# Two gated transformer blocks on one core: one region of 1024 slot rows per expert, and a new order around the routing

## The chip, the cores and the metric

The kernel runs on one core of a Trainium2 chip. The metric is the device time of one execution in microseconds (us). The engines of the core are named as in the profile: PE is TensorE (PEld its weight loads), DVE VectorE, ACT ScalarE, POOL GpSimd and SP SyncE, which here only issues DMAs.

## What is computed

The input is 2 batches of 512 tokens with 256 features. Cut to what matters:

```
xn = layernorm(x)
s  = attention0(xn)                     # 16 heads, 4 key/value heads, rotary
g  = silu(ffn0(xn))                     # gate/up/down, inner size 1024
x  = x + s * g
xn = layernorm(x)
# branch: linear attention
Q, K, V = split(xn @ W_in.T + b_in)     # 256 -> 768
Q, K = rope(Q), rope(K)
A  = sum over tokens of (K / |K|) * V   # one row per batch
s  = (A * Q) @ W_out.T + b_out + xn
# experts: top-1 of 8
route = sigmoid(xn @ router_w); e = argmax(route); prob = max(route)
g  = silu(prob * (silu(xn @ gate_w[e]) * (xn @ up_w[e])) @ down_w[e])
x  = x + s * g
```

## The kernel before

Token tiles have 128 tokens: 8 in all (NT), 4 per batch (TB). Each engine runs its own instruction list in order, and semaphores tie the lists together.

**Attention part.** A planner, `attention_plan`, writes one list of items (scores, row maxima, probabilities, values, and the gate, up and down products of block 0 as filling), and every engine walks that list for its own share. Small steps are put at a step and quarter by `due(step, quarter, item)`; a small cost table (`Clock.PE`, `other`) decides how much filling goes in front of an item whose inputs it believes late. Batch 0 gets its second layernorm, the transposes `rows_T` and its router logits inside this part (steps 19 to 22), batch 1 at its end. PSUM bank 5 (`misc`) is shared by the small steps through the semaphore `misc_free`. The list ends with the products `qkv1` of W_in for the four tiles of batch 0, with `rope1(0)` and with the logits of batch 1.

**Routing.** After the list DVE routes all 8 tiles at once (L1181 to L1216): probability, one-hot, a running sum over tiles, and after two PE products ("counts", L1559 and L1560) the row of every token. Token rows are packed: an expert starts at the first tile after the previous expert's last one, so the row of any token depends on the totals of all 1024. Then POOL scatters the 8 token tiles into DRAM (`xs_dram`, "slot_rows", 15 x 128 rows) with 8 indirect DMAs (L779). At its start SP has filled this area once with rows that carry no token (`in_empty`).

**Expert tiles.** SP waits for all 8 scatters and loads 8 slot tiles, one DMA each with a fixed address (L677), then releases the weights of experts 0 to 2, which it had loaded before, and issues the loads of experts 3 to 7 (L687). PE's `tile(i)` reads the expert's number from `tile_e`, makes the gate (L1600), the transposes of the tile before (L1576), up (L1608), the transposes of the next slot rows (L1568) and the down product of the tile before (L1586). The inputs need 11 expert tiles. ACT makes the tanh of each tile (L960), copies transposes out of PSUM (L942, L948) and DVE multiplies (L1279, L1283, L1270, L1273). POOL scatters each result.

**Branch.** Between the plan and the first expert tile PE makes the W_in products of batch 1 (L1382; bank pair 6 and 3 in turns, freed by DVE's bias addition L1035), the transposes of Q (`q_T`, L1622, copied out by ACT L936), the token sum of batch 0 (L1631) and `branch(0)`, `branch(1)` (L1643). `side_work(i)` puts the rest behind expert tiles 0 to 3: key norms and token sum of batch 1, `branch(2)`, `branch(3)`. ACT's squares of the keys (L862) wait for the rotation of their batch. `keep_warm` are transposes without use.

## Time and profile before

| | us |
|---|---|
| median of 3 runs | 370.25 |
| lowest, highest | 370.02, 370.71 |
| span of the profiled execution | 370.6 |
| PE busy in it | 326.3 (88%) |
| DVE busy | 239.2 (65%) |
| ACT busy | 154.4 (42%) |
| POOL busy | 62.8 (17%) |

The profiled execution has a span of 370.6 us and nothing is reported around it, so it stands 0.35 us above the median. Times in the text are counted from the start of the span. The span has three parts: the attention part up to about 250, the stretch between it and the first expert tile (250 to 280.5), and the expert tiles with the output (280.5 to the end). A row of the chain of waits is one piece of the work that ended last; a row of the timeline is one or a few instructions of an engine, with the idle time before them and what ended it in brackets.

### The profile page before, as it was taken

The page shows a single profiled execution, that of the slowest core. Times are in us where ns is not written, and L with a number is a line of the kernel's source. Part 1 is how long each engine was busy: PE and PEld are TensorE (multiplying, and loading weights), DVE is VectorE, ACT ScalarE, POOL GpSimd, SP SyncE. Part 2 cuts the span into 40 slices and gives each one's busy share as a digit, 9 for nine tenths or more (in the row PEclk, how much of TensorE's full clock was granted, in tenths as well). Part 3 has the DMA queues.
Part 4 walks back from the last instruction along what each step waited for, and adds up shares of the span by engine and source line. Part 5 has one row for each costly group of instructions (what it writes and reads, how often), then busy time and mean ns, then how long its engine had stood idle before and what let it go on. Part 6 is the DMA issues. An engine that isn't in the chain of part 4 may idle for free.

```text
span 370.6 us, 4637 instructions
## 1 busy us (share of the span) xinstructions
PE 326.3 (88%) x1598; PEld 191.5 (52%) x1598; DVE 239.2 (65%) x473; ACT 154.4 (42%) x279; POOL 62.8 (17%) x64
## 2 busy tenths in 40 slices
PE   3849859999999999999999999989968999999730
PEld 3426636545555454455554555556554576666420
DVE  3999895977666677877958510499793644433305
ACT  1614722476766655553664555203113322332300
POOL 4372480000011000000000000014570111211211
PEclk9958997999999999999999999996998999999965
DMA  7960000000000000000000050093029960111015
GB/s 262 405 161 0 2 0 3 0 3 1 0 4 0 3 0 3 0 0 3 2 2 1 0 171 2 2 371 138 31 92 329 435 240 30 30 42 44 17 44 200
DMA packets 9914, 28.46 MB, mean 77 GB/s; under 512 B 1342, under 2 KB 6559, under 8 KB 8608
## 3 DMA queue, kind: packets, MB, share of 16 engines
q1 hardware_dynamic: 8976, 26.01, 19.3%
q0 software_dynamic: 912, 2.12, 1.5%
q8 instruction: 15, 0.25, 0.3%
q14 instruction: 11, 0.09, 0.1%
HBM read 24.86 MB, written 5.55 MB: 82 GB/s over the span
## 4 chain that ended last, share of the span: by engine, by line
PE 72%; DVE 17%; DMA 4%; issue 2%; POOL 2%; ACT 1%; DVEq 0%; SPq 0%; POOLq 0%
PE ps L1532 11%; PE ps L1477 8%; PE ps L1445 8%; PE ps L1545 7%; PE ps L1467 7%; PE ps L1586 6%; PE ps L1600 6%; PE ps L1608 5%; PE ps L1382 3%; DVE xn L1014 3%; PE ps L1407 2%; DVE nmax L1069 2%; POOL slot_rows L779 2%; PE ps L1361 2%; PE ps L1576 1%
## 5 line engine op out<-in xcount | busy, mean ns | idle before, releaser
L1069 DVE TENSOR_REDUCE nmax<-ps 128x1 f32<-128x512 f32 x128 | 85.8, 688 | 34.4 <-PE ps L1445 33.7
L880 ACT ACTIVATE shared<-ps 128x512 f32<-128x512 f32 x128 | 74.2, 594 | 53.9 <-PE ps L1467 52.8
L1445 PE MATMUL ps<-experts 96*128 96x512 bf16 x128 | 48.2, 384 | 1.8 <-DVE experts L1076 1.2
L1467 PE MATMUL ps<-experts 99*128 99x512 bf16 x128 | 48.5, 382 | 0.0
L1545 PE MATMUL ps<-shared,experts 128*128 128x256 f32 x128 | 38.0, 386 | 0.0
L1477 PE MATMUL ps<-shared,experts 128*32 128x512 f32 x256 | 34.1, 605 | 0.3 <-ACT shared L880 0.3
L1445 PEld LDWEIGHTS ps<-experts 96*128 96x128 bf16 x128 | 12.5, 98 | 36.8 <-DVE nmax L1069 18.2
L1545 PEld LDWEIGHTS ps<-shared,experts 128*128 128x128 f32 x128 | 23.3, 191 | 9.7 <-issue 3.4
L1382 PE MATMUL ps<-late_weights,xnT 128*128 128x512 f32 (+1 forms) x64 | 25.0, 542 | 0.7 <-DVE shared L1035 0.7
L769 POOL TENSOR_TENSOR experts<-experts,late_weights 128x768 f32<-128x768 f32 x1 | 1.8, 1809 | 130.9 <-ACT experts L870 130.9
L888 ACT ACTIVATE experts<-ps 96x1024 bf16<-96x1024 bf16 x18 | 18.0, 1020 | 12.5 <-PE ps L1407 12.4
L1586 PE MATMUL ps<-experts,shared 128*128 x88 | 22.5, 402 | 0.8 <-ACT shared L948 0.8
L1600 PE MATMUL ps<-experts,xsT 128*128 x44 | 22.1, 627 | 0.7 <-ACT xsT L942 0.7
L1608 PE MATMUL ps<-experts,xsT 128*128 x44 | 20.7, 593 | 0.0
L1532 PE MATMUL ps<-xnT,late_weights 128*128 128x512 f32 x48 | 19.6, 407 | 0.0
L1382 PEld LDWEIGHTS ps<-late_weights,xnT 128*128 128x128 f32 x64 | 13.1, 213 | 10.6 <-issue 8.8
L1586 PEld LDWEIGHTS ps<-experts,shared 128*128 128x128 f32 x88 | 16.9, 203 | 3.1 <-issue 1.0
L1467 PEld LDWEIGHTS ps<-experts 99*128 99x128 bf16 x128 | 12.4, 98 | 9.9 <-issue 3.5
L1279 DVE SCALAR_TENSOR_TENSOR gated<-tanh_g,ps 128x512 f32<-128x512 f32 x11 | 7.6, 687 | 13.1 <-ACT tanh_g L960 13.1
L1128 DVE SCALAR_TENSOR_TENSOR gx<-gated,ps 128x256 f32<-128x256 f32 x8 | 3.4, 421 | 18.5 <-ACT gated L917 18.4
L1344 PE MATMUL ps<-wl,xnT 128*128 128x384 f32 x32 | 12.7, 557 | 1.8 <-DVE xnT L1028 1.2
L954 ACT ACTIVATE late_weights<-late_weights 128x256 f32<-128x256 f32 x11 | 4.6, 417 | 22.9 <-DVE late_weights L1270 22.9
(204 smaller groups left out, 536.3 us busy)
## 6 DMA issues: line engine op xcount, KB each, us to landing
experts<-in_experts SPq DMA_DIRECT2D x8, 1536.0 KB, 10.6
shared<-in_wgu SPq DMA_DIRECT2D x1, 2048.0 KB, 11.1
slot_rows<-in_empty SPq DMA_DIRECT2D x1, 1950.0 KB, 19.6
late_weights<-slot_rows SPq DMA_DIRECT2D x9, 130.0 KB, 2.3
x<-in_x SPq DMA_DIRECT2D x2, 512.0 KB, 5.7
shared<-in_wdn SPq DMA_DIRECT2D x1, 1024.0 KB, 13.1
shared<-expert_results SPq DMA_DIRECT2D x4, 256.0 KB, 3.7
out_x<-x SPq DMA_DIRECT2D x4, 256.0 KB, 2.0
```

The costliest lines, as they stand in the source:

```text
L880: nc.scalar.activation(probs[:, n % 2, hh, :], ps[:, 2 + hh % 2, :], ACT.Exp, scale=float(HD) ** -0.5).then_inc(s["exp_done"], 1)
L888: nc.scalar.activation(dst, src.rearrange("p (h s) -> p h s", h=2), ACT.Copy).then_inc(s["misc_free" if b else "stack_copied"], 1)
L1069: nc.vector.tensor_reduce(nmax[:, 4 * t + hh:4 * t + hh + 1], ps[:, m % 2, :], AX, ALU.max, negate=True).then_inc(s["max_done"], 1)
L1382: last = nc.tensor.matmul(bank[:, a, 0:hi - lo], xnT[:, k, P * j:P * j + P], win[:, k, lo:hi], start=k == 0, stop=k == KD - 1)
L1445: nc.tensor.matmul(ps[:, m % 2, :], qs[0:KS, b, GR * g + hh, P * t:P * t + P], ks[0:KS, b, g, :], start=True, stop=True).then_inc(s["score ...
L1467: nc.tensor.matmul(ps[:, 2 + hh % 2, :], ks[0:KM, b, g, P * t:P * t + P], qs[0:KM, b, GR * g + hh, :], start=True, stop=True).then_inc(s[" ...
L1477: last = nc.tensor.matmul(ps[VW * hh:VW * hh + VW, 4, :], vaug[:, TB * b + t, g, :], probs[:, n % 2, hh, :], start=t == 0, stop=t == TB - 1)
L1532: ins = nc.tensor.matmul(ps[:, bk, :], w_parts[w_], x_parts[x_], start=k == 0 and n_ == 0, stop=k == KD - 1 and n_ == 2)
L1545: ins = nc.tensor.matmul(ps[:, bk, 0:D], hT[:, i, P * (j % TB):P * (j % TB) + P], wdn[:, i, :], start=i == 0, stop=i == NI - 1)
L1586: last = nc.tensor.matmul(ps[:, 6, 0:D], hmT[:, i % 2, P * k:P * k + P], Wm[:, bass.ds(base[i] + 2 * KD * EI + D * k, D)], start=k == 0, s ...
L1600: last = nc.tensor.matmul(ps[:, i % 2, :], xsT[:, i % 2, P * k:P * k + P], Wm[:, bass.ds(base[i] + EI * k, EI)], start=k == 0, stop=k == K ...
L1608: last = nc.tensor.matmul(ps[:, 2 + i % 2, :], xsT[:, i % 2, P * k:P * k + P], Wm[:, bass.ds(base[i] + EI * (KD + k), EI)], start=k == 0, ...
```

## The change

- `xs_dram` grows to 8 regions of 1024 rows, one per expert (8192 rows). A token's row is its expert's region plus the tokens of that expert before it, so batch 0 needs nothing of batch 1. It is routed (`route`, three stages), counted (`counts`) and given rows (`place_rows`) at steps 23 and 24 of the attention part, and POOL scatters its 4 tiles then. The empty rows are written in four DMAs of 2048 rows, each after the row-maxima DMAs of one of the first four units.
- After the plan only batch 1 is routed: 4 tiles, with the totals of batch 0 as its start. PE's counts come one W_in product earlier (after tile 4, not after tile 5). The last step of `rope1(0)` moves behind the routing on DVE. DVE now makes the rows, then all tables of tiles (14 instructions, two tables more: `tile_r` is the first slot row of each expert tile), and only then the bias addition of tile 4.
- POOL makes the second scatter before the product of keys and values and the key norms of batch 0.
- SP reads `tile_r` into a register for each slot tile and loads the rows at this address. It waits for the tables and the scatters; slot tiles 3 to 7 wait for the last W_in product (all waited for it before).
- PE makes the fourth W_in product of batch 1 straight after the third, then `q_T(0)` and `q_T(1)`. `q_T(2)`, `q_T(3)` and the token sum of batch 0 go behind expert tile 0, `branch(0)` behind tile 1, `branch(1)` and the token sum of batch 1 behind tile 2, `branch(2)` behind tile 3, `branch(3)` behind tile 4. `q_T(2)` and `q_T(3)`, the token sums and all branches use PSUM bank 7; `q_T(3)` waits until ACT has copied `q_T(2)`.
- ACT makes the squares of batch 1's keys and the last two Q copies after the tanh of tile 0. DVE adds up the tokens of batch 0 (`sum_tiles(0)`) and scales W_out (`scaled_output(0)`) in tile 0, does the key norms of batch 1 in tile 1.

```diff
-SLOTS = MT * P
+REGION = TOK
+SLOTS = E * REGION
+EMPTYINGS = 4
...
-                           (21, 2, ("rows_T", 0, 0)), (22, 0, ("rows_T", 0, 1)), (22, 2, ("logits", 0))):
+                           (21, 2, ("rows_T", 0, 0)), (22, 0, ("rows_T", 0, 1)), (22, 2, ("logits", 0)),
+                           (23, 1, ("route", 0, 0)), (23, 3, ("route", 0, 1)), (24, 1, ("route", 0, 2)), (24, 3, ("counts", 0)),
+                           (24, 3, ("place", 0))):
...
-    return {0: [("norm", 1)], 1: [("sum", 1)], 2: [("branch", 2)], 3: [("branch", 3)]}.get(i, [])
+    return {0: [("squares", 1), ("sum_tiles", 0), ("q_T", 2), ("q_T", 3), ("sum", 0)], 1: [("norm", 1), ("branch", 0)],
+            2: [("branch", 1), ("sum", 1)], 3: [("branch", 2)], 4: [("branch", 3)]}.get(i, [])
...
             def load_rows(i):
-                sp.dma_start(slot_row(i), xs_dram[P * i:P * i + P, :]).then_inc(x_sem[i % XR], 16)
+                row = sp.value_load(tile_r[0:1, i:i + 1], min_val=0, max_val=SLOTS - P)
+                sp.dma_start(slot_row(i), xs_dram[bass.ds(row, P), :]).then_inc(x_sem[i % XR], 16)
...
+                    sp.wait_ge(s["tile_experts"], 1)
                     sp.wait_ge(s["scattered"], 16 * NT)
-                    sp.wait_ge(s["qkv1_psum"], NT)
                     for i in range(XR):
+                        if i == 3:
+                            sp.wait_ge(s["qkv1_psum"], NT)
                         load_rows(i)
                     for a in range(FIRST_EXPERTS):
                         expert_here(a)
...
+            scatter(0)
             pool.wait_ge(s["qkv1_copied"], 1)
             pool.wait_ge(s["layer1_loaded"], 64)
             nc.gpsimd.tensor_tensor(qkv1[0][:, 1, :], qkv1[0][:, 1, :], bin_b, ALU.add).then_inc(s["bias_added"], 1)
             pool.wait_ge(s["bias_added"], 1)
+            scatter(1)
             key_times_value(0)
...
+            def place_rows(b, bank, read):
+                dve.wait_ge(s["counts"], b + 1)
...
+                nc.vector.tensor_copy(smi[:, TB * b:TB * b + TB], at8).then_inc(s["slots"], 1)
+                if b == 0:
+                    nc.vector.tensor_copy(small[:, 2, 0:E], bank[:, TB * E:PAIRS]).then_inc(s["tot0"], 1)
+                    dve.wait_ge(s["tot0"], 1)
+                    nc.vector.tensor_tensor(region1, small[:, 2, 0:E], const("region"), ALU.add).then_inc(read, 1)
...
+            for stage in range(3):
+                route(B - 1, stage)
+            rope1(0, 1)
+            place_rows(B - 1, ps[:, 5, :], None)
...
+            nc.vector.tensor_scalar_min(tile_r[:], at_row, float(SLOTS - P)).then_inc(s["tile_experts"], 1)
+            qkv1_bias(TB)
...
             whole_qkv(TB)
+            counts(B - 1, ps[:, 5, :])
             whole_qkv(TB + 1)
-
-            pe.wait_ge(s["onehot"], 1)
-            nc.tensor.matmul(ps[:, 5, 0:NT * E + E], const("before"), onehot, start=True, stop=False)
-            nc.tensor.matmul(ps[:, 5, 0:NT * E + E], const("ones"), before_tile(3), start=False, stop=True).then_inc(s["counts"], 1)
             whole_qkv(TB + 2)
...
                 if n == B * KD - 1:
-                    pe.wait_ge(s["acol_ready"], 1)
+                    pe.wait_ge(s["qT_ready"], n)
...
+            whole_qkv(TB + 3)
             q_T(0)
             q_T(1)
-            whole_qkv(TB + 3)
-            token_sum(0)
-            pe.wait_ge(s["qkv1_ready"], biased(NT - 2))
-            branch(0)
-            branch(1)
-            q_T(2)
-            q_T(3)
             pe.wait_ge(s["qkv1_ready"], biased(NT - 1))
-            pe.wait_ge(s["qT_ready"], B * KD)
-            pe.wait_ge(s["slots"], 1)
             keep_warm(ROWS_WARM, 3)
             rows_T(0)
             keep_warm(TILE_WARM, 3)
```

PE before, from the third W_in product of batch 1 to the first expert tile (L1382 W_in, L1622 Q transposes, L1631 token sum, L1643 branch, L1323 keep_warm, L1568 slot rows):

```order
L1382 MATMUL ps<-late_weights,xnT 128x256 x2
L1622 MATMUL ps<-cst,experts 128x128 x8
L1382 MATMUL ps<-late_weights,xnT 128x512 x2
L1382 MATMUL ps<-late_weights,xnT 128x256 x2
L1631 MATMUL ps<-cst,shared 128x1 x2
L1643 MATMUL ps<-shared,xnT 128x256 x8
L1622 MATMUL ps<-cst,shared 128x128 x8
L1323 MATMUL ps<-cst 128x128 x4
L1568 MATMUL ps<-cst,xs 128x128 x2
L1323 MATMUL ps<-cst 128x128 x8
```

PE now, the same place and the end of expert tile 0 (L1446 W_in, L1692 Q transposes, L1703 token sum, L1387 keep_warm, L1638 slot rows, L1678 up):

```order
L1446 MATMUL ps<-late_weights,xnT 128x256 x2
L1692 MATMUL ps<-cst,experts 128x128 x8
L1387 MATMUL ps<-cst 128x128 x4
L1638 MATMUL ps<-cst,xs 128x128 x2
L1387 MATMUL ps<-cst 128x128 x8
...
L1678 MATMUL ps<-experts,xsT 128x512
L1638 MATMUL ps<-cst,xs 128x128 x2
L1692 MATMUL ps<-cst,shared 128x128 x8
L1703 MATMUL ps<-cst,shared 128x1 x2
```

Token sum, branches and the second half of the Q transposes have left the place ahead of the first tile; the transposes and the token sum stand behind tile 0.

ACT before, from the Q copies (L936) over the first slot-row copy (L942), the squares of batch 1 (L862, L863) to the tanh of tile 0 (L960):

```order
L936 ACTIVATE xnT<-ps 128x512 x4
L942 ACTIVATE xsT<-ps 128x256
L862 ACTIVATE wl,st<-shared 128x256 x4
L863 ACTIVATE st<-st 128x4
L960 ACTIVATE tanh_g<-ps 128x512
L942 ACTIVATE xsT<-ps 128x256
L960 ACTIVATE tanh_g<-ps 128x512
```

ACT now (L960 Q copies, L966 slot-row copies, L984 tanh, L886 and L887 squares):

```order
L960 ACTIVATE xnT<-ps 128x512 x2
L966 ACTIVATE xsT<-ps 128x256
L984 ACTIVATE tanh_g<-ps 128x512
L966 ACTIVATE xsT<-ps 128x256
L886 ACTIVATE wl,st<-shared 128x256 x4
L887 ACTIVATE st<-st 128x4
L960 ACTIVATE xnT<-ps 128x512 x2
L984 ACTIVATE tanh_g<-ps 128x512
```

The squares and two Q copies stand between the tanh of tile 0 and that of tile 1.

SP now, the slot-row loads 2 and 3; before, each was one DMA:

```order
L693 TENSOR_LOAD tile_r
L693 ISA x2
L694 ISA
L694 DMA xs<-slot_rows 128x260
L693 TENSOR_LOAD tile_r
L693 ISA x2
L694 ISA
L694 DMA late_weights<-slot_rows 128x260
```

Each DMA has gained a register load and three register instructions ahead of it.

## Rows read from the trace of the kernel before

**Rows 1.** The page: busy time, share of the span, instructions.

```profile
PE 326.3 (88%) x1598; PEld 191.5 (52%) x1598; DVE 239.2 (65%) x473; ACT 154.4 (42%) x279; POOL 62.8 (17%) x64
```

**Rows 2.** Chain that ended last, 250 to 320: start us, us, what.

```profile
253.33 8.14 PE ps L1382 x16
...
264.25 0.18 DVE smi L1216
...
264.71 1.19 POOL slot_rows L779
...
274.20 2.43 DMA slot_rows<-xn,smi
...
276.64 2.08 DMA xs<-slot_rows
...
280.53 3.12 PE ps L1600 x4
...
285.62 0.39 ACT xsT L942
...
286.25 1.98 PE ps L1600 x4
...
292.33 0.34 PE ps L1631 x4
...
306.15 1.73 PE ps L1643 x8
307.88 1.72 PE ps L1600 x4
...
313.69 1.72 PE ps L1600 x4
```

**Rows 3.** Timeline of PE around 200: start us, us, line, operation.

```profile
200.84 0.39 PE L1445 MATMUL ps<-experts 96*128 96x512 bf16 x1
...
202.37 0.60 PE L1485 MATMUL ps<-cst,xs 128*128 128x128 f32 x4
```

**Rows 4.** Windows of 2 us: busy us of each engine, then granted clock, DMA share, GB/s.

```profile
254.00:256.00 2.00, 2.00 (x4) 0.79 (x3) 1.90 (x5) 0.99 (x4) 0.91 (x1) 0.50 0.00 0
...
280.00:282.00 2.00, 2.00 (x5) 0.97 (x4) 0.00 (x0) 1.75 (x8) 0.00 (x0) 0.50 0.87 252
```

**Rows 5.** Timeline of DVE, routing and tables.

```profile
253.72 1.23 DVE L1055 TENSOR_TENSOR experts<-shared 128x1024 f32<-128x1024 f32 x1
...
255.92 1.60 DVE L1184 TENSOR_TENSOR small<-small,xn 128x64 f32<-128x64 f32 x1
...
262.17 0.22 DVE L1203 TENSOR_TENSOR small<-small,cst 128x64 f32<-128x64 f32 x1
...
265.10 1.81 DVE L1035 TENSOR_TENSOR shared<-ps,late_weights 128x768 f32<-128x768 f32 x2
```

**Rows 6.** Timeline of POOL, product of keys and values.

```profile
255.09 2.35 POOL L764 TENSOR_TENSOR shared<-experts 128x1024 f32<-128x1024 f32 x1 [9.22 <-DVE experts L1055]
```

**Rows 7.** Timeline of SP's queue, slot-row loads.

```profile
277.97 2.33 SPq L677 DMA_DIRECT2D late_weights<-slot_rows  x5
```

**Rows 8.** Timeline of ACT, tanh of tiles 7 and 8.

```profile
327.09 0.60 ACT L960 ACTIVATE tanh_g<-ps 128x512 f32<-128x512 f32 x1 [0.78 <-PE ps L1600]
...
332.91 0.60 ACT L960 ACTIVATE tanh_g<-ps 128x512 f32<-128x512 f32 x1 [0.78 <-PE ps L1600]
```

**Rows 9.** Timeline of PE, Q transposes, a branch pair, first slot rows.

```profile
264.33 1.04 PE L1622 MATMUL ps<-cst,experts 128*128 128x128 f32 x8
...
270.76 3.69 PE L1643 MATMUL ps<-shared,xnT 128*128 128x256 f32 x16 [1.28 <-DVE shared L1035]
...
278.77 0.44 PE L1568 MATMUL ps<-cst,xs 128*128 128x128 f32 x2 [1.88 <-DMA xs<-slot_rows]
```

**Rows 10.** Timeline of ACT, Q copies and the squares of batch 1.

```profile
275.00 1.16 ACT L936 ACTIVATE xnT<-ps 128x512 f32<-128x512 f32 x2 [8.96 <-PE ps L1622]
...
279.52 0.41 ACT L862 ACTIVATE wl<-shared 128x256 f32<-128x256 f32 x1
...
281.67 0.20 ACT L863 ACTIVATE st<-st 128x4 f32<-128x4 f32 x1
```

**Rows 11.** Timeline of DVE, key norms and token sum of batch 1.

```profile
286.08 0.16 DVE L639 TENSOR_SCALAR st<-st 128x4 f32<-128x4 f32 x1
...
288.63 1.53 DVE L1232 SCALAR_TENSOR_TENSOR shared<-shared,st 128x256 f32<-128x256 f32 x3
```

More of the change, by code:

```diff
@@ L59, in const_columns @@
               ("cos1", TB * ROT), ("sin1e", TB * ROT // 2), ("sin1o", TB * ROT // 2),
-              ("desc", E), ("full", NT), ("lower", E * E), ("tile_id", MT), ("token", NT)]
+              ("desc", E), ("full", NT), ("lower", E * E), ("tile_id", MT), ("token", NT), ("region", E), ("tile_row", MT)]
     at, out = 0, {}
@@ L182, in run @@
             self.done[("moved", item[1])] = self.now["act"] + self.ROWS_MOVED
+        elif kind == "place":
+            self.other("dve", 1.4, ("misc",), t)
+        elif kind == "route":
+            self.other("dve", .8, ("route",))
         elif kind in ("heads_norm", "wo"):
@@ L765, in key_times_value, with scatter @@
                                         ).then_inc(s["kv_ready"], 1)
+            def scatter(b):
+                pool.wait_ge(s["slots"], b + 1)
+                pool.wait_ge(s["slots_emptied"], 16 * EMPTYINGS)
+                pool.wait_ge(s["rows_norm"], NT + TB * (b + 1))
+                for j in range(TB * b, TB * b + TB):
+                    nc.gpsimd.indirect_dma_start(
+                        out=xs_dram[:, :], out_offset=bass.IndirectOffsetOnAxis(ap=smi[:, j:j + 1], axis=0),
+                        in_=xn[:, j, :], in_offset=None).then_inc(s["scattered"], 16)
+            scatter(0)
             pool.wait_ge(s["qkv1_copied"], 1)
@@ L972, in _ @@
             key_squares(0)
-            for n in range(B * KD):
+            for n in range(KD):
                 q_copy(n)
             xsT_copy(0)
-            key_squares(1)
             for i in range(SURE):
                 tile(i)
+                for kind, n in side_work(i):
+                    if kind == "squares":
+                        key_squares(n)
+                    elif kind == "q_T":
+                        q_copy(n)
             n_tiles = act.value_load(tiles_n[0:1, 0:1], min_val=SURE, max_val=MT)
@@ L1192, in _ @@
-            nc.vector.tensor_tensor(before_tile(3), before_tile(2), before_tile(2, 4), ALU.add).then_inc(s["onehot"], 1)
-            qkv1_bias(TB)
-            cnt = small[:, 2, 0:72]
-            tot = small[:, 2, 64:72]
-            dve.wait_ge(s["counts"], 1)
-            chain(nc.vector.tensor_copy(cnt, ps[:, 5, 0:72]))
-            big = lg.rearrange("p (e k) -> p e k", e=E)
+                    rope1(it[1], it[2])
+                elif kind == "route":
+                    if it[2] == 0:
+                        dve.wait_ge(s["late_loaded"], 32)
+                    route(it[1], it[2])
+                elif kind == "place":
+                    row_tails(it[1])
+                    place_rows(it[1], misc, s["misc_free"])
+                elif kind == "routing_start":
+                    row_tails(B - 1)
@@ L1218, in _ @@
+            chain(nc.vector.tensor_reduce(column(tiles), b3, AX, ALU.add))
+            chain(nc.vector.tensor_tensor(b3, const("lower").rearrange("p (e k) -> p e k", e=E), row(tiles).to_broadcast([P, E, E]), ALU.mult))
+            chain(nc.vector.tensor_reduce(column(base), b3, AX, ALU.add))
+            nc.vector.tensor_scalar(skip, tiles, -float(P), float(REGION), ALU.mult, ALU.add)
+            chain(nc.vector.tensor_tensor(end, base, tiles, ALU.add))
             te = tanh_g[:, 0, 0:MT * E].rearrange("p (i e) -> p i e", i=MT)
@@ new lines, in _ @@
+            at_row = tanh_g[:, 0, 288:288 + MT]
+            chain(nc.vector.tensor_tensor(te, column(const("tile_id")).to_broadcast([P, MT, E]), row(end).to_broadcast([P, MT, E]), ALU.is_ge))
+            nc.vector.tensor_reduce(column(tr), te, AX, ALU.add)
+            chain(nc.vector.tensor_tensor(rows, te, row(skip).to_broadcast([P, MT, E]), ALU.mult))
+            nc.vector.tensor_scalar_min(tile_e[:], tr, float(E - 1))
+            chain(nc.vector.tensor_reduce(column(at_row), rows, AX, ALU.add))
@@ L1385, in qkv, with counts @@
                     last.then_inc(s["qkv1_psum"], 1)
+            def counts(b, bank):
+                pe.wait_ge(s["onehot"], b + 1)
+                nc.tensor.matmul(bank[:, 0:PAIRS], const("ones"), earlier(2), start=True, stop=False)
+                nc.tensor.matmul(bank[:, 0:TB * E], const("before"), onehot, start=False, stop=True).then_inc(s["counts"], 1)
             for it in plan:
                 kind = it[0]
-                if kind == "stack_T":
+                if kind == "counts":
+                    misc_bank(it)
+                    counts(it[1], misc)
+                elif kind == "stack_T":
                     _, b, c = it
```

164 lines of the change are left out of this document (87 added, 77 removed).

## The prediction

> **What bounds the kernel now.** I read the page first: PE is busy 88% of the span and no other engine over 65% [rows 1], so a change must take work off PE or close its holes. Then the windows of 2 us for the granted clock, and last the chain of waits, which says who closes each hole. Up to 250 the chain lies almost wholly on PE. From 253.33 it runs through two W_in products (8.14 us for 16 matmuls, most of it at the low clock: the window at 254 has 0.50) [rows 2, 4], through DVE's tables to the slot numbers (264.25 to 264.43), then through POOL: eight scatters start between 264.71 and 274.20, one every 1.36 us, the last lands after 2.43, the slot rows after 2.08 more, and the first expert tile starts at 280.53 [rows 2]. PE has its holes here; what it does meanwhile (W_in, Q, branches) does not decide the end. From 280.53 on PE is the chain again.
>
> So there are two accounts. Whatever is taken out between 253 and 280 counts until PE itself, or SP, is the last to be ready; whatever is put behind expert tiles counts in full, because PE is the chain there.
>
> **Attention part: +1.2 us.** The two small count matmuls cost about 0.3 (the four of a token sum take 0.34 [rows 2]). The real price is the in-order list of DVE. Route and place of batch 0 are about 19 small DVE instructions at 0.23 each (nine of them take 262.17 to 264.25, 2.08 us, in the routing before [rows 2, 5]), so some 4.4 us in the stretch 195 to 204, where DVE also makes the row maxima on which PE's scores wait: PE already waited for one until 200.84 [rows 3]. Two new waits are PE's own: counts(0) needs the one-hot, and the head transposes (L1485, at 202.37 before [rows 3]) need bank 5, which place_rows frees only with its last instruction. Placing DVE's instructions one after the other, the head transposes start at 205.25; four down products (0.87) and the counts have been moved ahead of them, which leaves 2.7 - 1.2 = 1.5 late, and part comes back where the fill was. I take +1.2 with ends +0.3 (only the matmuls) and +2.7 (nothing comes back). The four emptying DMAs go from DRAM to DRAM right behind row DMAs with some 18 us to the next ones; zero. The scatter of batch 0 finds POOL idle; zero.
>
> **Ahead of the first tile.** Times on the old scale, 1.2 to be added. DVE: the last step of the rotation (1.23 from 253.72 [rows 5]) is out of the way, so routing starts at 253.7 instead of 254.9; L1184, 1.60 before, ran while POOL's key product held from 255.09 for 2.35 [rows 5, 6] and should be 0.2 with that product behind the scatter. One-hot at 256.1. PE: one W_in product from 253.33 at the low clock is 5.1, counts done 258.8. Place_rows needs 4 instructions: slots at 259.75 (before 264.43). POOL: four scatters, the last starting 3 x 1.36 + 0.3 later at 264.2, landed 266.6 (before 276.63). That is 10 us.
>
> But three others are late now. *DVE's tables* stand ahead of the bias of tile 4: 14 instructions x 0.23 = 3.2, tables at 262.95, bias done 263.9 (0.9 each [rows 5]). PE has finished the next product at 261.6 and waits 2.3 us for it, since the third product reuses its banks. *PE*: third and fourth product 2.6 each at full clock, 263.9 to 269.2; two Q transposes 1.0 [rows 9], four warm ones, slot rows, eight warm ones (1.33): tile 0 could start at 272.55. A hole of 2.3 us is larger than the one before 278.77 (1.88 [rows 9]), after which the clock stood at 0.50 in the window at 280 [rows 4]. There the four gate matmuls took 3.12 against 1.72 at full clock [rows 2], so a low stretch costs about 1.4 to 1.8. I take one here: W_in done at 270.9, PE ready at 274.2. *SP*: slot rows 3 to 7 wait for the last W_in product, and the weights of experts 0 to 2 are released only behind all eight loads. A load cost 0.47 to issue (five in 2.33 [rows 7]). Now each has a register load ahead of it, which the trace never times. The nearest rows bound it: between tanh of tiles 7 and 8 ACT reads the tile count into a register, and its idle time before is 0.78 with it and 0.78 without it [rows 8]. It fits in 0.78, at least zero. I take the middle, 0.4: five loads 4.3, from 270.9 to 275.3. Tile 0 starts at 275.3, the range of this term being 272.55 (load free, clock full) to 277.2 (0.78). Gain **5.2**, where the scatters alone promised 10.
>
> The Trainium skill has a price for that load ("DMA: Bandwidth & Descriptors", Latency and other measured facts: a floor of about 600 ns for a tensor_load). By it five loads would be 5.3, tile 0 would start at 276.2, and the total below would be 0.9 higher; no row here times it.
>
> **Expert tiles.** *Work moved in:* four Q transpose groups of 128 columns twice, 8 matmuls (0.9), token sum 0.34, two branches of 1.73 [rows 2, 9]: 4.7 us that lay in holes and now lie on the chain. *A new wait in tile 0.* Count from its start at full clock: gate and up 3.44, slot rows of tile 1 until 3.66, q_T(2) until 4.1. q_T(3) must wait for ACT's copy of q_T(2) (one bank now), and ACT has the slot-row copy until 4.1 and then the squares of batch 1, 279.52 to 281.87, 2.35 us [rows 10]; its copy ends at 7.0. q_T(3) to 7.5, its copy to 8.1, and the token sum, on the same bank, to 8.45. Tile 1 starts 8.5 after tile 0. PE stands still for 3.5 of that. *Tile 2:* DVE does key norms and token sum in a row (286.08 to 290.16, 4.1 us [rows 11]) and branch(0), 1.4, before the product of tile 2; branch(1) is then read late and the token sum of batch 1 waits 1.1. *Total:* tile 5 starts at 8.5 + 4 x 5.82 + four branches 6.9 + token sum 0.34 + wait 1.1 = 40.2 after tile 0. Before: 313.69 - 280.53 = 33.2 [rows 2], with 1.4 of low clock and a wait of 0.65 (the slot-row copy at 285.62) in it. Cost **+7.0**. *Clock:* 3.5 us of standing still in tile 0 again is more than the hole that lowered the clock before; one low stretch over tile 1, **+1.7** (0 to 3.4, if the wait before tile 0 lowers it too). From tile 5 on nothing changes: 5.82 a tile, same end.
>
> **Sum.** +1.2 - 5.2 + 7.0 + 1.7 = +4.7. The span of the profile is 370.6 and the median 370.25; on the median 374.95, I say **375.0**.
>
> **Rivals.**
> *A, even.* The holes do not lower the clock and the register load is nearly free: tile 0 at 272.55, -8.0 + 7.0 + 1.2 = +0.2: 370.5. For it: the hole of 1.28 before 270.76 [rows 9] lowered nothing. Against it: that in tile 0 is nearly three times as long.
> *B, faster.* The same front, and the chain finds slack in the attention part, so that DVE's extra work costs only its 0.3: -8.0 + 7.0 + 0.3 = -0.7, 369.5; if the squares also ended before q_T(2) the wait of 3.5 would go and it would be 366. It decides from a front gain of over 7.3. Against it: ACT's list puts the squares behind the tanh of tile 0, so the wait is built in.
> *C, the loads are dear.* Register load and address take over 1.2 us a piece: five of them 8.3, tile 0 at 279.3, +1.2 - 1.2 + 7.0 + 3.1 = +10: 380. For it: they are four more instructions per row; against it: ACT's 0.78.
> *D, the change does not move the scatter.* If POOL's second scatter waited for the emptying or for batch 0's, the front would stay at 280: +9. The emptying is issued 100 us before; little speaks for it.
>
> **How the numbers follow.** Forecast (slower by 2 to 8) 0.62, A 0.13 (half of it within the bound), B 0.13, C and D 0.12. Range: low 369.4 takes in A and most of B, high 378.8 is the forecast with the dear end of the load (+1.9) and a second low stretch (+1.7). A measurement of this kernel tells 0.2%, 0.7 us, from no change. Faster by over 0.2%: 0.12; within: 0.10; slower: 0.78.
>
> **What would show it.** In the profile after: second scatters from about 261 and landed by 268; DVE's bias of tile 4 behind the tables and PE idle some 2 us before the third W_in product; SP's slot loads 0.9 apart, the last at 276; gate of tile 0 about 276.5 (275.3 + 1.2); PE idle 3.5 between q_T(2) and the token sum with ACT's squares as the releaser; tile 5 some 41 after tile 0. If tile 0 starts before 273, or tile 1 follows in under 6 us, the forecast is wrong and the kernel is even or faster; if SP's loads lie over 1.5 apart, C is right.

## The result and the profile after

The changed kernel takes 383.39 us (median of 4 runs, 381.28 to 383.65), the kernel before 370.42 beside it: a ratio of 1.034 (95% interval 1.030 to 1.038, taken on the means), slower by 13.0 us on the medians. The prediction had the direction and 375.0; the time lies 4.6 us above its upper end.

The page of the changed kernel, with the span, what answers to [rows 1], and two groups of its table (busy us, mean ns, then the idle time before them and what ended it):

```profile
span 381.8 us, 4754 instructions
PE 330.0 (86%) x1602; PEld 192.5 (50%) x1602; DVE 236.5 (62%) x493; ACT 154.5 (40%) x279; POOL 65.3 (17%) x65
...
L1670 PE MATMUL ps<-experts,xsT 128*128 x44 | 24.4, 684 | 5.5 <-SPq L690 4.7
L1446 PE MATMUL ps<-late_weights,xnT 128*128 128x512 f32 (+1 forms) x64 | 24.8, 538 | 2.2 <-DVE shared L1063 2.2
```

PE does 3.7 us more in time (330.0 for 326.3) with only four more matmuls, so nearly all of the surplus is the clock and not work. The gate products (L1670) stood 4.7 us behind SP's release of the experts' weights, the W_in products 2.2 behind DVE's bias.

The stretches between fixed places of PE's list, from the two profiled executions (start of batch 0's router logits, of batch 1's, of the gate of tile 0, of the gate of tile 5, end):

| stretch | before | after | difference | predicted |
|---|---|---|---|---|
| start to logits of batch 0 | 189.68 | 188.94 | -0.74 | 0 |
| to logits of batch 1 | 61.20 | 63.27 | +2.07 | +1.2 |
| to gate of tile 0 | 29.62 | 26.15 | -3.47 | -5.2 |
| to gate of tile 5 | 33.03 | 46.30 | +13.27 | +8.7 |
| to the end | 57.07 | 57.14 | +0.07 | 0 |
| span | 370.6 | 381.8 | +11.2 | +4.7 |

The first row is no effect: in the eleven profiles of this study those logits start anywhere from 188.94 to 190.04.

**Ahead of tile 0.** The chain of waits of the changed kernel (start us, us, what; cut to the pieces that matter), which answers to [rows 2] from 264 on:

```profile
262.21 0.99 POOL slot_rows L793
...
266.03 2.54 DMA slot_rows<-xn,smi
268.65 0.48 SPq L693
269.64 0.35 SPq L694
...
270.77 0.34 SPq L694
...
277.82 0.33 SPq L694
278.36 3.78 PE ps L1670 x4
282.14 2.70 PE ps L1678 x4
```

The last scatter lands at 268.57, as intended 8 us earlier than before (276.63). Then SP alone is the chain for 9.7 us: eight slot-row loads, each a register load (L693) and a DMA (L694), 1.1 us from one to the next (once 1.56, between the fifth and the sixth), where the kernel before needed 0.47 [rows 7]. The weights of experts 0 to 2 are released behind the eighth. PE had been ready since 273.6. Its timeline there (start us, us, line, operation, idle time before), which answers to [rows 9], and through tiles 0 and 1:

```profile
260.40 2.83 PE L1446 MATMUL ps<-late_weights,xnT 128*128 128x512 f32 x8
265.40 5.43 PE L1446 MATMUL ps<-late_weights,xnT 128*128 128x512 f32 x16 [2.18 <-DVE shared L1063]
...
272.59 1.04 PE L1387 MATMUL ps<-cst 128*128 128x128 f32 x8
278.36 3.78 PE L1670 MATMUL ps<-experts,xsT 128*128 x4 [4.73 <-SPq L690]
281.93 2.91 PE L1678 MATMUL ps<-experts,xsT 128*128 x4
284.68 0.38 PE L1638 MATMUL ps<-cst,xs 128*128 128x128 f32 x2
284.89 0.60 PE L1692 MATMUL ps<-cst,shared 128*128 128x128 f32 x4
288.37 0.63 PE L1692 MATMUL ps<-cst,shared 128*128 128x128 f32 x4 [2.87 <-ACT xnT L960]
289.68 0.61 PE L1703 MATMUL ps<-cst,shared 128*128 128x1 f32 x4 [0.69 <-ACT xnT L960]
290.64 3.64 PE L1670 MATMUL ps<-experts,xsT 128*128 x4 [0.36 <-issue]
...
308.48 0.61 PE L1703 MATMUL ps<-cst,shared 128*128 128x1 f32 x4 [0.78 <-DVE gx L1314]
```

**Tiles.** Tile 1 starts 12.28 us after tile 0 (before: 5.75). Three things make up the 6.5 us. Gate and up of tile 0 took 6.3 us at the lower clock; they take 3.5 at full clock and took 4.7 in the kernel before, so this is 1.6. PE stood still for 2.87, 0.69 and 0.36 us around the second Q transpose and the token sum, 3.25 more than before. And the Q transposes and the token sum themselves, which now lie here, are 1.6. ACT's timeline shows whom it waited for: the copy of the first Q transposes (L960 at 287.64) stands behind four squares (L886) and their sums. It answers to [rows 10].

```profile
285.38 0.41 ACT L886 ACTIVATE wl<-shared 128x256 f32<-128x256 f32 x1
...
287.53 0.21 ACT L887 ACTIVATE st<-st 128x4 f32<-128x4 f32 x1
287.64 0.58 ACT L960 ACTIVATE xnT<-ps 128x512 f32<-128x512 f32 x1
```

The granted clock of the same stretches (busy us of each engine, then the clock as a share of full speed), which answers to [rows 4]:

```profile
278.00:280.00 2.00, 1.64 (x2) 0.84 (x3) 0.00 (x0) 0.00 (x0) 0.46 (x1) 0.50 0.80 197
...
292.00:294.00 2.00, 2.00 (x3) 0.57 (x2) 0.00 (x0) 0.00 (x0) 0.00 (x0) 0.50 0.99 424
```

So there are two low stretches in these tiles, 1.2 GHz both, one over tile 0 and one over the gate of tile 1. PE had stood still for 4.73 us ahead of the first, and for 3.9 us in three pieces ahead of the second.

**Attention part.** DVE's timeline: the row maxima (L1148), on which PE's scores wait, now share the engine with the routing of batch 0.

```profile
195.11 1.29 DVE L1148 TENSOR_REDUCE nmax<-ps 128x1 f32<-128x512 f32 x2
196.31 0.16 DVE L1111 TENSOR_SCALAR xn<-xn 128x4 f32<-128x4 f32 x1
...
201.11 0.20 DVE L1119 TENSOR_TENSOR ranks<-ranks 128x40 f32<-128x40 f32 x1
```

From 194.1 to 201.5 the chain of waits lies wholly on DVE. PE was idle there 0.55 us for a row maximum and 0.37 for the one-hot (L1119).

### The profile page after: what moved, and what is told of

Same layout as the page of the kernel before. It is cut to its first block, busy times and chain, and to the rows that moved or that the text cites. A ratio compares the mean times of both kernels' runs of the same rounds, so it can differ in the third digit from the quotient of the medians.

```text
span 381.8 us, 4754 instructions
## 1 busy us (share of the span) xinstructions
PE 330.0 (86%) x1602; PEld 192.5 (50%) x1602; DVE 236.5 (62%) x493; ACT 154.5 (40%) x279; POOL 65.3 (17%) x65
## 4 chain that ended last, share of the span: by engine, by line
PE 69%; DVE 18%; issue 4%; DMA 4%; ACT 2%; SPq 2%; POOL 1%; DVEq 0%; POOLq 0%
PE ps L1605 10%; PE ps L1550 8%; PE ps L1518 7%; PE ps L1618 7%; PE ps L1540 6%; PE ps L1670 6%; PE ps L1656 5%; PE ps L1678 5%; DVE nmax L1148 3%; DVE xn L1042 3%; PE ps L1480 2%; PE ps L1446 2%; PE ps L1408 2%; PE ps L1425 2%; PE ps L1646 1%
## 5 line engine op out<-in xcount | busy, mean ns | idle before, releaser
L1148 DVE TENSOR_REDUCE nmax<-ps 128x1 f32<-128x512 f32 x128 | 85.5, 688 | 32.9 <-PE ps L1518 32.2
L1518 PEld LDWEIGHTS ps<-experts 96*128 96x128 bf16 x128 | 12.5, 97 | 37.3 <-DVE nmax L1148 18.5
L1670 PE MATMUL ps<-experts,xsT 128*128 x44 | 24.4, 684 | 5.5 <-SPq L690 4.7
L1446 PE MATMUL ps<-late_weights,xnT 128*128 128x512 f32 (+1 forms) x64 | 24.8, 538 | 2.2 <-DVE shared L1063 2.2
L793 POOL DMA_INDIRECT slot_rows<-xn,smi x8 | 7.9, 989 | 108.0 <-DVE smi L1130 106.2
L1678 PE MATMUL ps<-experts,xsT 128*128 x44 | 21.7, 618 | 0.0
L1446 PEld LDWEIGHTS ps<-late_weights,xnT 128*128 128x128 f32 x64 | 12.8, 208 | 12.0 <-issue 8.6
L984 ACT ACTIVATE tanh_g<-ps 128x512 f32<-128x512 f32 x11 | 6.6, 597 | 29.2 <-PE ps L1670 29.2
```

What stands on the lines that cost most here:

```text
L1148: nc.vector.tensor_reduce(nmax[:, 4 * t + hh:4 * t + hh + 1], ps[:, m % 2, :], AX, ALU.max, negate=True).then_inc(s["max_done"], 1)
L1446: last = nc.tensor.matmul(bank[:, a, 0:hi - lo], xnT[:, k, P * j:P * j + P], win[:, k, lo:hi], start=k == 0, stop=k == KD - 1)
L1518: nc.tensor.matmul(ps[:, m % 2, :], qs[0:KS, b, GR * g + hh, P * t:P * t + P], ks[0:KS, b, g, :], start=True, stop=True).then_inc(s["score ...
L1670: last = nc.tensor.matmul(ps[:, i % 2, :], xsT[:, i % 2, P * k:P * k + P], Wm[:, bass.ds(base[i] + EI * k, EI)], start=k == 0, stop=k == K ...
L1678: last = nc.tensor.matmul(ps[:, 2 + i % 2, :], xsT[:, i % 2, P * k:P * k + P], Wm[:, bass.ds(base[i] + EI * (KD + k), EI)], start=k == 0, ...
```

## The experiments

Each kernel is the changed one with the edit shown. All medians stand beside 370.4 to 370.5 for the kernel before. The theory: three causes, the slot-row loads on SP in front of the release (R), the squares in front of the Q copy (Q), the routing in the attention part in a place where DVE is short (V), and the lower clock that the first two bring with them. The rival in each case is that something else stands there as late, or that the clock takes back what a wait gives.

**Release first.**

```diff
+                    for a in range(FIRST_EXPERTS):
+                        expert_here(a)
                     sp.wait_ge(s["tile_experts"], 1)
                     sp.wait_ge(s["scattered"], 16 * NT)
                     for i in range(XR): ...
-                    for a in range(FIRST_EXPERTS):
-                        expert_here(a)
```

> The changed kernel, but SP releases the weights of experts 0 to 2 before it issues the slot-row loads, not after all eight. Theory R (the eight loads, each with its register load, 1.12 us apart, hold tile 0 from 273.6, when PE is ready, to 278.4): tile 0 starts at 273.6 to 274, the loads still end near 278, the gate of tile 0 takes 1.7 and not 3.8 us because PE has not stood still for 4.7 us before it, and the time falls by 5 to 8 us against the changed kernel's 383.4. Rival (the slot rows themselves, or the tables, come late and the release is only the last of several): tile 0 moves by under 1 us and the time stays within 1 us of 383.4.

Measured 376.57 us (375.99 to 379.62), 6.8 under the changed kernel, in the expected range. The timeline of PE:

```profile
274.35 1.98 PE L1670 MATMUL ps<-experts,xsT 128*128 x4
...
283.86 3.78 PE L1670 MATMUL ps<-experts,xsT 128*128 x4
```

Tile 0 starts with no idle time before it, 4.0 us earlier, and at full clock. The slot loads still run until 277.4, as far apart as before, and nobody waits for them: it was their place ahead of the release that cost. The hole of 2.87 behind the squares and the slow gate of tile 1 are untouched. Between the two profiles the spans differ by 7.7: 4.6 is the way from batch 1's logits to tile 0 and 2.8 the clock of tile 0, both of them the edit's; 1.1 is lost on a longer low stretch over tile 1, and 1.7 gained because the last down product ran at full clock, which the edit need not have caused.

**Row numbers as constants** (the release still behind the eight loads; the constants are the rows that these inputs lead to):

```diff
-                        load_rows(i)
+                        row = (0, 128, 1024, 2048, 2176, 3072, 4096, 5120)[i]
+                        sp.dma_start(slot_row(i), xs_dram[row:row + P, :]).then_inc(x_sem[i % XR], 16)
```

> The first eight loads of slot rows take their row numbers as constants (those that the inputs of this case lead to: 0, 128, 1024, 2048, 2176, 3072, 4096, 5120) in place of a register each; all else is as in the changed kernel, the release still behind the eight loads. Theory R (the register loads on the queue's engine are what holds the release): the loads are 0.45 to 0.55 us apart in place of 1.12, the five behind the last W_in product end by 273.4, tile 0 starts at 273.8 to 274.6 in place of 278.4, near where the prediction had it: 378 to 380 us. Rival (the 1.12 is the price of a load that reads rows just scattered by another queue, with a register or without): spacing stays over 0.9, tile 0 after 276.5, 382 to 384 us.

Measured 377.19 us (374.41 to 377.54), 6.2 under the changed kernel and 0.8 below the expected range; tile 0 starts where it was expected. SP's queue and PE:

```profile
268.81 1.28 SPq L713 DMA_DIRECT2D xs<-slot_rows  x3
271.12 2.23 SPq L713 DMA_DIRECT2D late_weights<-slot_rows  x5
```

```profile
273.98 1.98 PE L1671 MATMUL ps<-experts,xsT 128*128 x4
```

The loads are 0.45 us apart, so the 1.1 was not the reading of freshly scattered rows: the register load and its three register instructions cost 0.66. Tile 0 starts at 273.98 in place of 278.36, 21.51 us after batch 1's logits; with the early release it is 21.54, and in both PE comes to tile 0 without a wait. Both edits remove the same wait, and give the same.

**Every register loaded twice:**

```diff
                 row = sp.value_load(tile_r[0:1, i:i + 1], min_val=0, max_val=SLOTS - P)
+                row = sp.value_load(tile_r[0:1, i:i + 1], min_val=0, max_val=SLOTS - P)
```

> The changed kernel with the register load of each slot-row address done twice. It prices that load. Theory R: the spacing of SP's slot-row loads grows from 1.12 by the price of one load and its register instructions, about 0.65, to 1.77; tile 0 comes 8 x 0.65 = 5 us later and the time rises by 5 to 6 us. Rival (the spacing is that of a DMA whose address comes from a register, not of the load): spacing grows by under 0.2 and the time by under 2 us.

Measured 385.96 us (384.03 to 388.41), 2.6 over the changed kernel, less than expected. In its chain of waits a DMA follows the next after 1.65:

```profile
270.03 0.35 SPq L695
...
271.68 0.34 SPq L695
```

The second load with its register instructions thus costs 0.54 (expected 0.65), and tile 0 starts at 282.57. From the first of the eight DMAs to tile 0 it is 12.54 us, in the changed kernel 8.72: 3.8 more, which is seven steps of 0.54. That the time rose by less has its reason ahead of the loads: the first of them comes 15.76 us after the logits of batch 1, in the changed kernel 17.43, because that one had a long low stretch from 253 to 260 and this one none. The rival (the address, and not the load, is what costs) is out: it allowed the spacing to grow by under 0.2.

**Squares behind the Q copies:**

```diff
-    return {0: [("squares", 1), ("sum_tiles", 0), ("q_T", 2), ("q_T", 3), ("sum", 0)],
+    return {0: [("sum_tiles", 0), ("q_T", 2), ("q_T", 3), ("squares", 1), ("sum", 0)],
```

> The changed kernel, but ACT makes the squares of batch 1's keys behind the last two Q copies, not ahead of them. Theory S (the squares, 2.35 us, hold the copy that frees bank 7 for the second Q transpose and the token sum): the token sum comes 2.3 us earlier, tile 1 starts 10.0 us after tile 0 and not 12.3, and the low clock over the gate of tile 1 (3.64 us) goes, since PE stands still for about 1.3 us there and not 3.6: 2 to 4 us less than 383.4. Rival (PE would wait in tile 0 anyway, for DVE's sum of tokens or the rotation of batch 1): under 0.7 us.

Measured 377.99 us (376.11 to 378.88), 5.4 under the changed kernel, more than the expected 2 to 4. PE:

```profile
277.52 3.78 PE L1670 MATMUL ps<-experts,xsT 128*128 x4 [4.76 <-SPq L690]
...
287.79 1.98 PE L1670 MATMUL ps<-experts,xsT 128*128 x4 [0.40 <-issue]
```

The hole of 2.87 is 0.78 now, and tile 1 starts 10.27 after tile 0 instead of 12.28: 2.0, the size of the squares. A further 1.7 is the gate of tile 1, at full clock for once (1.98, not 3.64). The remaining 1.7 are the clock elsewhere: from batch 1's logits to tile 0 this execution needed 24.52 us and not 26.15, with a shorter low stretch over the W_in products, and the edit stands behind that place. The edit is worth 3.7 in this execution; the 1.7 of clock in it is not sure to come, as the kernel with three edits shows.

**More warming in front of tile 0** (`TILE_WARM` 8 to 36, so that PE is busy while SP loads):

```diff
-    ROWS_WARM, TILE_WARM = 4, 8
+    ROWS_WARM, TILE_WARM = 4, 36
```

> The changed kernel with 36 transposes without use between the first slot rows and tile 0, not 8, so that PE is busy until about 277.5 and not 273.6. It separates the clock from the waiting: tile 0 still cannot start before 278.4. Theory C (the standing still of 4.7 us lowered the clock, and gate and up of tile 0 took 6.5 us for 3.4): gate and up of tile 0 in 3.5 us, 3 us less than 383.4. Rival (the clock falls there for another reason, or the 3 us are taken back by the wait for ACT in tile 0): under 1 us.

Measured 381.15 us (379.41 to 382.28), 2.2 under the changed kernel; the two ranges overlap, so the trace has to say it. PE at tile 0:

```profile
277.57 1.98 PE L1670 MATMUL ps<-experts,xsT 128*128 x4 [0.29 <-SPq L690]
```

Tile 0 began with 0.29 idle and its gate took 1.98, up 1.88, and tile 1 follows after 9.60 us in place of 12.28: the low stretch over tile 0 came from the standing still, and is worth 2.7 to 2.8. But the gate of tile 1 (behind the hole of 2.87) took 3.78 as ever. Warming hides one consequence; the wait stays.

**Routing of batch 0 later** (steps 27 to 29 in place of 23 and 24):

```diff
-                           (23, 1, ("route", 0, 0)), (23, 3, ("route", 0, 1)), (24, 1, ("route", 0, 2)), (24, 3, ("counts", 0)),
-                           (24, 3, ("place", 0))):
+                           (27, 1, ("route", 0, 0)), (27, 3, ("route", 0, 1)), (28, 3, ("route", 0, 2)), (29, 3, ("counts", 0)),
+                           (29, 3, ("place", 0))):
```

> One part of the change alone is moved: routing, counts and placing of batch 0 stand three to five steps later in the attention part (steps 27 to 29 in the place of 23 and 24), where VectorE has gaps between the gated blocks. Theory V (what these 1.5 us of attention time are is VectorE work put between the softmax pieces it was needed for, 194 to 203.6): the logits of batch 1 end 0.8 to 1.5 us earlier than the 254.85 of the changed kernel, the rest stays: 381.5 to 382.6 us in the median. Rival W (the cost is that work wherever it stands, or it is in the two TensorE products of the counts and the emptying DMAs): no change beyond 0.5 us, 383.0 to 383.9, and the logits end at 254.5 to 255.

Measured 380.07 us (378.30 to 381.99), 3.3 under the changed kernel, below the expected range and overlapping the changed kernel's; the trace gives the edit less. PE at the counts, and at batch 1's logits:

```profile
223.64 0.31 PE L1454 MATMUL ps<-ranks,cst 128*128 128x40 f32 x2
...
251.28 3.17 PE L1501 MATMUL ps<-router,xnT 128*128 128x8 f32 x16 [0.25 <-ACT xnT L920]
```

No PE wait precedes the counts, and from batch 0's logits (189.65) to batch 1's it is 61.63 us, where the changed kernel has 63.27 and the kernel before 61.20. The stretch repeats well: the kernels with the early release, the squares last, more warming and constant rows have 63.25 to 63.27 there, and the next kernel, with the late routing, 61.63 again. So 1.64 of the 2.07 us were the place, and 0.43 is what stays, near the 0.36 that the count matmuls take here (223.64 to 224.00). The end of these logits was expected 0.8 to 1.5 us earlier than 254.85; it came at 254.3, because this execution made most of them at the lower clock. The rest of the 3.3 is spread between executions.

**All three edits** (release first, squares last, routing late):

> Three edits together: experts 0 to 2 are released before the slot rows are loaded, the squares of batch 1 stand behind the Q copies in tile 0, and batch 0 is routed at steps 27 to 29. Theory (the three causes are independent and lie one behind the other on the path): the release alone gave 6.8 us and the squares 5.4, of which 1.8 us each was one gate product at full clock, so they don't add in full: 383.4 - 6.8 - 2.5 - 1.0 = 373 us (370.5 to 375). Tile 0 starts at 273 to 274.4, tile 1 starts 8.0 to 9.5 us behind it. Rival (the clock takes back what the waits give: a gate or up product at the lower level turns up wherever a wait closes): 375.5 to 377, as with the release alone.

Measured 372.45 us (370.86 to 374.77), 10.9 under the changed kernel, in the expected range; the rival (375.5 to 377, the clock takes back what the waits give) is out in its time, though one gate product (3.39, of tile 1) did fall to the lower clock. Tile 0 starts at 272.34 and tile 1 after 7.62, both a little better than expected. What is left shows in PE's timeline:

```profile
264.03 5.43 PE L1446 MATMUL ps<-late_weights,xnT 128*128 128x512 f32 x16 [2.17 <-DVE shared L1063]
...
278.97 0.58 PE L1703 MATMUL ps<-cst,shared 128*128 128x1 f32 x4 [0.88 <-DVE shared L1297]
279.96 3.39 PE L1670 MATMUL ps<-experts,xsT 128*128 x4 [0.41 <-issue]
```

**And the bias of tile 4 ahead of the tables**, right behind the slot numbers:

```diff
             place_rows(B - 1, ps[:, 5, :], None)
+            qkv1_bias(TB)
             ...
             nc.vector.tensor_scalar_min(tile_r[:], at_row, float(SLOTS - P)).then_inc(s["tile_experts"], 1)
-            qkv1_bias(TB)
```

> As the kernel with the three edits, and the bias of token tile 4 is added ahead of the expert tables in place of behind them, so that TensorE's hole of 2.18 us at 262 to 264.4 (the next W_in product waits for that bank) closes; slots come before it, tables and release 0.95 us later. Theory H (the hole lets the clock down: the two W_in products behind it took 7.12 us in the run with the early release, 5.43 in the changed kernel): the W_in products end 3 to 5 us earlier, by 267; tile 0 is then bound by the slot rows (scatter lands at about 268.6, row 0 on chip at about 271, transposed and copied 1 us later) and starts 1.5 to 2.5 us earlier than in the kernel with the three edits: 368.5 to 371.5 us. Rival S (TensorE's front was not the last there; scatter and slot rows are already): same as the kernel with the three edits within 0.7 us, with TensorE idle in front of row 0.

Measured 370.74 us (369.42 to 373.12, 10 runs), ratio to the kernel before 1.0035 (0.9993 to 1.0078): no difference that can be told. PE:

```profile
265.41 2.85 PE L1446 MATMUL ps<-late_weights,xnT 128*128 128x512 f32 x8 [0.50 <-DVE shared L1063]
...
270.90 0.44 PE L1638 MATMUL ps<-cst,xs 128*128 128x128 f32 x2 [0.93 <-DMA xs<-slot_rows]
...
272.24 1.98 PE L1670 MATMUL ps<-experts,xsT 128*128 x4
```

The hole is 0.50 instead of 2.17, and from batch 1's logits (252.98) to tile 0 it is 19.26 us in place of 21.50. But most of these 2.24 us lie ahead of the edited place: the counts began 6.17 us after the logits and not 7.58, because the low stretch there was shorter in this execution. From the W_in product behind the counts (259.51) to tile 0 it is 12.73 us, before the step 13.31, so the edit gives 0.6 at this front. That is what rival S said (within 0.7, with PE idle in front of row 0), and not theory H. Whether the hole lets the clock down was not put to the test: in the kernel with three edits the two W_in products behind it took 5.43 us, full clock. Nor do the times settle it: the medians are 1.7 apart, but the ranges overlap, and the spans of the two profiles differ the other way (368.9 before the step, 369.8 with it). PE now waits 0.93 for the slot rows themselves, so what comes last at this front is the scatter and the load of the rows. The front is 10.4 us shorter than before the change. All of that is spent again: tile 1 starts 8.2 after tile 0, and the token sums wait.

**And the token sums one tile later:**

```diff
-    return {0: [("sum_tiles", 0), ("q_T", 2), ("q_T", 3), ("squares", 1), ("sum", 0)], 1: [("norm", 1), ("branch", 0)],
-            2: [("branch", 1), ("sum", 1)], 3: [("branch", 2)], 4: [("branch", 3)]}.get(i, [])
+    return {0: [("sum_tiles", 0), ("q_T", 2), ("q_T", 3), ("squares", 1)], 1: [("norm", 1), ("sum", 0)],
+            2: [("branch", 0)], 3: [("branch", 1), ("sum", 1)], 4: [("branch", 2)], 5: [("branch", 3)]}.get(i, [])
```

> As the kernel with the bias ahead of the tables, with the work beside the tiles spread by one more: both token sums come a tile later (batch 0's behind tile 1, batch 1's behind tile 3), and with them the branch products (tiles 2 to 5). Theory (what is left between that kernel and a lead over the kernel before are the waits of the token sums on VectorE: 1.45 + 0.40 us at batch 0's, 0.78 + 0.38 at batch 1's): tile 5 starts 2 to 3 us earlier than 40.5 behind tile 0, and the time is 368.3 us (367.3 to 369.5), 0.6% under the kernel before. Rival (VectorE's key norms, 16 small operations, then stand in front of tile 2's gated product and the wait moves there, or a gate product falls to the lower clock once more): 370 to 371.5 us, no difference to the kernel before.

Measured 367.46 us (366.46 to 368.49, 12 runs), ratio 0.994 (0.991 to 0.997): faster than the kernel before by 2.9 us on the medians and 2.2 by the ratio, as expected a small gain. PE:

```profile
278.08 1.98 PE L1670 MATMUL ps<-experts,xsT 128*128 x4 [0.35 <-issue]
...
284.00 0.50 PE L1703 MATMUL ps<-cst,shared 128*128 128x1 f32 x4
...
300.69 0.61 PE L1703 MATMUL ps<-cst,shared 128*128 128x1 f32 x4 [0.78 <-DVE gx L1314]
```

Tile 1 starts 6.1 us after tile 0 and batch 0's token sum waits for nothing. The second token sum kept its 0.78: it waits for DVE's reading of the branch product just ahead of it, which came along. Tile 5 starts 37.3 us after tile 0 in place of 40.5, but one branch product (1.7) is then still to come. By tile 6, where all side work is done in both, the gain is 1.46 us (44.87 against 46.33 after tile 0), less than the 2 to 3 expected. The rest of the 3.3 us in the medians is clock: the last down product took 1.99 here and 3.46 in the profile of the kernel before this step.

## Why the prediction was right or wrong

The step that failed is the price of the register load on SP (0.4 us taken, 0.66 measured), and with it the clock term, which counted one low stretch (+1.7) where there were two (4.6). The mechanisms were found in the trace, and the sizes were too small in four terms, all in the same direction.

- **Base.** The span of the profile, 370.6, was set beside the median of 370.25 as if they were one. In every run since, the time is 1.8 to 2.0 above the span (383.59 for 381.8), so the profiled execution of the kernel before lasted some 372.4 by this estimate. That is 2 us longer than its usual ones: 37 later executions of it have a median span of 368.6, and most have a mean granted clock of 0.946 to 0.964 where the profiled one has 0.942. A profile with more of the lower clock in it than usual makes the next kernel look 2 us better. That is the difference between +11.2 (spans) and +13.0 (medians). Which stretch of it was slower than usual stays open.
- **Attention, +1.2 predicted, +2.07 measured.** Right in kind: "the in-order list of DVE". The head transposes came when they were placed (205.0), but the part that "comes back where the fill was" did not come. (From 202.37 to 205.25 it is 2.9 us and not 2.7; and counted from batch 0's logits, which this execution started 0.74 earlier, the head transposes came 3.4 us later than before, with 2.2 us of down products and counts moved ahead of them.) The late routing shows that 1.64 of the 2.07 is place.
- **Scatters.** Nearly as predicted: from 262.2, the last at 266.03, landed at 268.57, where "landed by 268" was said. So rival D is out. The hole of 2.3 us behind DVE's tables was 2.18. It did not lower the clock there (5.43 for two W_in products); in the kernels with the early release, more warming and the late routing the same hole was followed by 7.12. So the low stretch expected at this place (+1.7) did not come; the one over 253 to 260 was in the prediction already, as the 5.1 us of the first W_in product.
- **The register load, the step that failed.** It was priced at 0.4, "the middle" between zero and 0.78, and cost 0.66. The bound of 0.78 held; the middle was a guess with no row behind it. The sum then counted five loads from the end of the last W_in product. What happened is the chain of all eight from the scatter's landing: 268.57 + 1.07 + 8.18 + 0.54 = 278.36, where the 8.18 are seven steps from one DMA to the next, and the W_in products were over at 270.8, before the third DMA was issued (271.87). That the chain was another one did little by itself, and that is luck, since the W_in products ended 1.3 us sooner than forecast. The same eight loads at the forecast 0.86 would have let tile 0 start at about 276.0 (an estimate from these numbers), and the forecast was 276.5. The 2.4 us between 276.0 and 278.36 are the price of the load, 0.45 for one longer step among the seven included. Rival C had the place and not the price: it asked for loads over 1.5 apart and tile 0 at 280.5, and they were 1.1 apart. The Trainium skill ("DMA: Bandwidth & Descriptors", Latency and other measured facts) puts a tensor_load at about 600 ns at the least. The 0.66, register instructions included, agrees with it; the second load in a row, 0.54 with its register instructions, lies a little under it. By the 600 ns the sum would have been 0.9 higher, still too low.
- **Tile 0's wait, +3.5 predicted, 3.92 measured** (2.87 + 0.69 + 0.36). Right, and right about the releaser; the kernel with the squares last shows that 2.0 of it were the squares.
- **Clock, +1.7 predicted for one low stretch over tile 1.** There were two: over tile 0 2.8 us (the release and the warming kernels show it gone), over tile 1's gate and the first transposes behind it some 1.8. The text had the second in brackets, "if the wait before tile 0 lowers it too", and with the wait at 4.73 us and not at 1.1 it did. It is the mis-sized register load a second time: 1.7 in tile 0's start, 2.8 in its clock. (The upper end of the range had this second stretch in it, at 1.7; the two additions there make 378.6 and not 378.8.)
- **Tile 2**, 9.0 predicted, 9.47 measured. From tile 5 on nothing changed, as stated.

Together 0.9 + 1.7 + 4.6 - 0.7 = 6.5 us on the spans, and 1.8 for the base. Rivals A and B are out: tile 0 started at 278.36 and not before 273. The 0.7 us that the prediction took as the least that can be told was too little: the kernel before has since been measured between 365.9 and 372.8. A change of 13 us does not depend on it.

The kernel with all five edits also tells what the idea was worth: scattering batch 0 early, with the new order around it, does take 10 us from the front, as the prediction said of the scatters alone, but 6.0 of them come back behind the expert tiles (44.87 us from tile 0 to tile 6, before the change 38.85) and 0.4 in the attention part; the rest is a gain only when no new wait stands in PE's list.

## What to carry to other kernels

When a wait is shortened, list everything that fires behind it in order, and ask of each instruction on that queue who waits for its end: a signal that needs none of the loads ahead of it belongs in front of them (6.8 us for one moved loop). Work moved from a hole onto the critical engine is free only as long as the engines that serve it (here ACT's squares and DVE's token sums) are ordered by who is waiting, and a hole of some microseconds on TensorE can be paid twice, in time and in the clock after it. Compare a profile's span with the spans of other executions before using it as the base.

## What the runs showed of the hardware that was not expected

- A DMA on SP whose address comes from a register loaded just before costs 1.1 us of the queue, one with a constant address 0.45, one with two register loads 1.65. In the kernels that load the rows by register, one of the steps between the eight took some 0.45 longer than the others (1.56 in the changed kernel); why is open.
- Small POOL operations of 0.2 us took up to 1.2 while DVE ran its rotation (273.20 is the end of the first POOL operation, 273.15 that of the first DVE one). In the changed kernel, POOL and then DVE:

```profile
272.01 1.19 POOL L644 TENSOR_TENSOR st<-st 128x4 f32<-128x4 f32 x1
273.28 0.52 POOL L640 TENSOR_TENSOR st<-st 128x4 f32<-128x4 f32 x1
```

```profile
271.92 1.23 DVE L1083 TENSOR_TENSOR shared<-shared,cst 128x1024 f32<-128x1024 f32 x1
273.06 0.69 DVE L1084 TENSOR_TENSOR shared<-shared,cst 128x512 f32<-128x512 f32 x1
```

  Four POOL operations in a row end 0.05 to 0.06 us after a DVE one does; the same operations took 0.2 before DVE's rotation began. Nobody waited for them here.
- The same place gets a different clock in different executions and kernels, and the hole in front of it doesn't settle which. The third and fourth W_in product of batch 1 stand behind a hole of 2.17 to 2.19 us in seven kernels: they took 5.43 us in four of them and 7.12 in three. With the early release:

```profile
264.35 7.12 PE L1446 MATMUL ps<-late_weights,xnT 128*128 128x512 f32 x16 [2.18 <-DVE shared L1063]
```

  The last down product took 1.99 us where PE had idled 1.18 and 1.03 ahead of the transposes in front of it (early release, all five edits), but 3.67 behind 1.06 (late routing). The gate of tile 1 took 3.39 us in the kernel with three edits and 1.98 in the next, where PE had stood still a little longer in tile 0 (0.78 + 1.45 against 0.78 + 0.88) but less in front of the W_in products. In three of the eleven profiles the clock stood at 0.66 to 0.70 from 194 to 198, which cost 1.1 to 1.3 us; one of the three (two register loads) has the same attention part as the changed kernel, which stood at full clock there. The 37 executions of the kernel before go from 365.9 us at a mean granted clock of 0.963 to 372.8 at 0.941, and the longer ones mostly have the lower clock. So the steps above are read from stretches of the trace and not from the medians alone. What decides the clock of a place stays open.
